# A post-norm transformer layer on one core: maxima rows turned by a transposing DMA, and block 0's output products cut in column halves

## The chip, the cores and the metric

The kernel runs on one core of one Trainium2 chip. The metric is device time in microseconds (us) of one execution; lower is better. Five engines work side by side, each through its own queue in program order: PE (TensorE, matrix products; it reads SBUF and writes the eight banks of PSUM), ACT (ScalarE), DVE (VectorE), POOL (GpSimd) and SP (SyncE), which here only issues DMAs. They wait for each other by semaphores alone.

## The reference

`x` is 2 x 1024 x 512. The layer is attention with residual and layer norm, then a feed-forward stage with residual and layer norm. Only the attention matters here:

```python
qk = (x @ Wqk_w.T + Wqk_b).reshape(b, n, H, E, 2)      # H = 8 heads, E = 8
scores = jnp.einsum('bhqd,bhkd->bhqk', q, k)           # 1024 x 1024 for each head
attn = jax.nn.softmax(scores, axis=-1) / 64 ** 0.5
out = jnp.einsum('bhsl,bhlv->bhsv', attn, v)           # heads joined, then out @ Wo_w.T + Wo_b
x = _layernorm(x + attention(x)); x = _layernorm(x + ffn(x))
```

The feed-forward part has int4 weights with a scale for each group of 128 inputs, and an inner width of 1792. Any true maximum may be taken off a row of scores before the exponential; the kernel takes it off inside the product of the scores, as three more rows of operands.

## The kernel before

The 2048 tokens are four blocks `u` of 512. The eight heads are two groups of four (`NG = 2`), so there are eight groups `f = 2u + g`. A group has eight steps, one for each 128 keys; a step `n` (0 to 63; group `f` starts at step `8f`) has two pairs of heads, `pair` 0 and 1.

**First pass.** `first_pass` (L1040) computes scores of 128 queries by 512 keys into a ring of three PSUM banks (4, 5, 7; `RING`), and DVE reduces each to a maximum (`reduce`, L1356, recorded at L1361). There are 32 such products for each group, 256 in all, and they run ahead of the second pass: 46 come before step 0, then two behind each pair (`firsts_at`), until step 52. When a group's 32 maxima are there, DVE combines them (`combine`, L1364, recorded at L1371) into `mx`.

**Maxima into rows.** POOL splits `mx` into three half-precision parts `mp` (`split_max`, L577). PE turns them at pair 1 of step `8f - 3` (`turn_maxima`, L1057), ACT copies the turned rows out of PSUM to `mrows` (`max_out`, L829), and SP writes them by two DMAs (`max_rows`, L454, recorded at L466) into the operand rows of the group's queries (`qs`). The first scores of group `f`, at step `8f`, wait for that (`s_mld`, L1119).

**Second pass.** For each pair PE computes `scores` (L1112, recorded at L1132) into one of two alternating pairs of banks (0/1 and 2/3), ACT takes the exponential of both banks (`exps`, L814), and PE multiplies by the values one step later, in two halves of the queries (`av`, L1149, recorded at L1161), in bank 6.

**Turns.** Some other uses share the scores' two bank pairs, each in its place in the alternation (`turns_at`, L280): `M` (maxima), `avT` (the sums of group `f`, turned at step `8f + 9`, L1092; ACT copies them, POOL divides them in `normalise`, L660), and for block 0 `attT` (step 20, L1100) and the two output products `wo` (steps 22 and 23, L1108), each copied by ACT into `wob` (L842). In the step behind a turn the first-pass products go ahead of the scores (`firsts_ahead`). From step 53 (`DRAIN`) on the first pass is over and the products of blocks 1 and 2 use banks 4 and 7 instead.

**POOL's order** is written out by hand (L680 on): for each `f` from 2, `normalise(f - 2)`, `split_max(f)`, additions of the bias, loads of the weights (`load_weights`), and behind `f = 3` the four additions of block 0's attention to `x1` (`add_attention`, L646, recorded at L651). **SP's order** too: `max_rows(1)`, twelve DMAs that place rows of the second batch, the load of half of `x` (L483, 2 MB), `max_rows(2)`, the load of the other half (L489), `max_rows(3)`, and so on.

Of the kernel before, what the change touches and what calls it, by code (L numbers as in the profile page):

```python
# [16 lines left out]
F32 = mybir.dt.float32  # L17
# [40 lines left out]
def build(nc, x, xT, wqkT, bqk, wvT, bv, woT, bo, gq, gs, uq, us, dq, ds, ds_next, spread, out):  # L58
    ctx = ExitStack()
    with ctx:  # L60
# [76 lines left out]
        mp = sb("mp", [P, 2, 3 * HG * BT], F16)  # L137
        mrows = sb("mrows", [3 * HG * BT, 2, P], F16)
# [58 lines left out]
        s_m0 = sem("first_max_turn_read")  # L197
        s_of = sem("turn_full")
# [81 lines left out]
        def turns_at(n, pair):  # L280
# [3 lines left out]
            f, r = divmod(n + 3, KT)  # L284
            if r == 0 and f < NB * NG:
                return [("M", f, 0)]
            f, r = divmod(n - 9, KT)
# [3 lines left out]
            if r == 4:  # L291
                return [("attT", 0, 0)]
# [4 lines left out]
        WO_AT = (6, 7)  # L297
# [127 lines left out]
        def _(sp):  # L425
# [110 lines left out]
        def _(pool):  # L536
# [24 lines left out]
            nc.gpsimd.memset(stack[1][:].bitcast(F32), 0.0).then_inc(s_fill, 1)  # L561
            pool.wait_ge(s_fill, 4)
# [14 lines left out]
            def split_max(f):  # L577

                part = [mp[:, f % 2, :].rearrange("p (j i q) -> p i j q", j=2, i=3)[:, i, :, :] for i in range(3)]
                top = mx[:, f % 2, :].rearrange("p (j q) -> p j q", j=2)  # L580
                rest = mres[:].rearrange("p (j q) -> p j q", j=2)
                pool.wait_ge(s_mxc, f + 1)
# [97 lines left out]
            for f in range(2, NB * NG):  # L680
                normalise(f - 2)
                split_max(f)
# [8 lines left out]
                if f == 3:  # L691
                    for t in range(BT):
                        add_attention(0, t)
# [65 lines left out]
        def _(act):  # L759
# [63 lines left out]
            def first_max_out():  # L823

                act.wait_ge(s_rf, ring_count("M", 0))
                nc.scalar.activation(mrows[:, 0, :], ring_bank("M", 0)[0:3 * HG * BT, :].bitcast(F16)[:, 0:P],
                                     ACT.Copy).then_inc(s_m0, 1)

            def max_out(f):  # L829

                act.wait_ge(s_of, turn_count["M", f, 0])
                if f >= 2:
                    act.wait_ge(s_mld[f % NG], 16 * 2 * (f // NG))
                src = bank[shared_banks("M", f, 0)][0:3 * HG * BT, :].bitcast(F16)[:, 0:P]
                nc.scalar.activation(mrows[:, f % 2, :], src, ACT.Copy).then_inc(s_read, 1)
# [20 lines left out]
            def turn_out(kind, u, k):  # L856
# [6 lines left out]
                if kind == "M":  # L863
                    max_out(u)
# [111 lines left out]
        def _(pe):  # L976
# [80 lines left out]
            def turn_maxima(f, dst):  # L1057

                pe.wait_ge(s_mrow, f + 1)
                return nc.tensor.transpose(dst[0:3 * HG * BT, :].bitcast(F16)[:, 0:P], mp[:, f % 2, :], ident16[:])  # L1060
# [580 lines left out]
```

## Time and profile before

| | |
|---|---|
| median of 3 runs | 515.65 us (515.52 to 516.02) |
| the profiled execution | 515.38 us |
| its span, first to last instruction | 513.5 us |
| mean granted TensorE clock | 0.996 of full speed |
| PE busy | 499.5 us |
| DVE busy | 408.8 us |
| ACT busy | 406.8 us |
| POOL busy | 282.9 us |

The attention's second pass runs from about 50 us to about 211 us of the span, the feed-forward stage from there to the end. A row such as "L1161 PE MATMUL ... x832" groups instructions by line; on PE `x8` in a row stands for four fp32 products, which are recorded twice.

### The profile page before, as it was taken

The numbers are of one execution on the slowest core, as the hardware profiler recorded it, in microseconds if no ns is written. First come the engines' busy times: TensorE is split into PE (matmuls) and PEld (weight loads), VectorE is DVE, ScalarE is ACT, GpSimd is POOL, SyncE is SP. The second block draws the span as 40 slices with busy tenths as digits, with TensorE's granted clock in tenths as the row PEclk, the third lists the DMA queues.
The fourth block names the chain that finished last, engine by engine and source line by source line (L and its number), as shares of the span: only waits on it lengthen the run. The fifth ranks groups of instructions, "written<-read, shape, count | busy, mean of one in ns | idle before, by whom it ended". The sixth has DMA issues, their size and how long they took to land.

```text
span 513.5 us, 8164 instructions
## 1 busy us (share of the span) xinstructions
PE 499.5 (97%) x2986; PEld 194.3 (38%) x2986; DVE 408.8 (80%) x688; ACT 406.8 (79%) x569; POOL 282.9 (55%) x330
## 2 busy tenths in 40 slices
PE   8999999999999999999999999999999999999994
PEld 3222233323333322334444444444444444444441
DVE  2799999989999996478778778778668666788676
ACT  1523889988998889868888888888888888888883
POOL 9200094854744444072664686676885874748741
PEclk9999999999999999999999999999999999999998
DMA  6510018953720007500031121130020020000022
GB/s 194 158 48 19 8 54 210 263 106 73 110 43 2 2 5 164 226 1 0 8 56 21 22 41 22 21 63 1 1 82 1 1 84 0 2 0 1 0 82 82
DMA packets 30151, 29.21 MB, mean 57 GB/s; under 512 B 19488, under 2 KB 21920, under 8 KB 29856
## 3 DMA queue, kind: packets, MB, share of 16 engines
q1 hardware_dynamic: 26544, 22.41, 15.2%
q0 software_dynamic: 3424, 6.03, 6.6%
q8 instruction: 23, 0.38, 0.3%
q10 hardware_dynamic: 144, 0.26, 0.1%
q14 instruction: 16, 0.13, 0.1%
HBM read 24.37 MB, written 4.23 MB: 56 GB/s over the span
## 4 chain that ended last, share of the span: by engine, by line
PE 88%; DVE 5%; ACT 3%; issue 1%; DMA 1%; SPq 0%; POOLq 0%; POOL 0%; DVEq 0%
PE ps L1184 19%; PE ps L1172 19%; PE ps L1263 18%; PE ps L1161 10%; PE ps L1054 8%; PE ps L1132 6%; PE ps L984 3%; ACT pbuf L814 3%; DVE mxh L1361 2%; PE ps L1108 1%; PE ps L1144 1%; DMA arena<-xT 1%; PE ps L1036 1%; PE ps L994 1%; PE ps L1092 1%
## 5 line engine op out<-in xcount | busy, mean ns | idle before, releaser
L1361 DVE TENSOR_REDUCE mxh<-ps 128x1 f32<-128x512 f32 x256 | 157.4, 683 | 4.9 <-PE ps L1054 4.0
L814 ACT ACTIVATE pbuf<-ps,gamma 128x1024 f32<-128x1024 f32 x128 | 137.2, 1115 | 15.4 <-PE ps L1132 12.2
L907 ACT ACTIVATE ps<-ps,ratio 128x512 f32<-128x512 f32 x167 | 105.9, 659 | 41.4 <-PE ps L1172 38.6
L1263 PE MATMUL ps<-wd,stack 128*128 128x512 f16 x440 | 129.7, 379 | 0.0
L1184 PE MATMUL ps<-arena,wu 128*128 128x512 f16 x448 | 115.3, 379 | 0.0
L1172 PE MATMUL ps<-arena,wg 128*128 128x512 f16 x448 | 115.3, 379 | 0.1
L1542 DVE TENSOR_TENSOR ps<-ps,stack 128x512 f32<-128x512 f32 x128 | 87.9, 695 | 32.2 <-PE ps L1263 30.3
L913 ACT ACTIVATE ps<-ps,ratio 128x512 f32<-128x512 f32 x156 | 99.0, 659 | 5.4 <-PE ps L1184 1.1
L709 POOL CAST stack<-pbuf 128x512 f16<-128x512 f32 x55 | 33.5, 609 | 74.4 <-DVE pbuf L1517 74.4
L1542 DVE TENSOR_TENSOR ps<-ps,pbuf 128x512 f32<-128x512 f32 x76 | 52.6, 696 | 23.2 <-PE ps L1263 22.4
L1161 PE MATMUL ps<-pbuf,arena 128*32 128x256 f32 x832 | 66.5, 391 | 0.5 <-ACT avt L821 0.2
L711 POOL TENSOR_TENSOR stack<-pbuf,stack 128x512 f16<-128x512 f32 x55 | 63.6, 1156 | 4.5
L1172 PEld LDWEIGHTS ps<-arena,wg 128*128 128x128 f16 x448 | 43.5, 98 | 54.4 <-issue 1.7
L1184 PEld LDWEIGHTS ps<-arena,wu 128*128 128x128 f16 x448 | 43.4, 98 | 54.2 <-DVE pbuf L1517 2.7
L1263 PEld LDWEIGHTS ps<-wd,stack 128*128 128x128 f16 x440 | 43.0, 98 | 52.1 <-DVE ps L1542 0.4
L1054 PE MATMUL ps<-stack 64*128 64x512 f16 x256 | 60.8, 382 | 1.3 <-DVE mxh L1361 0.6
L1132 PE MATMUL ps<-stack 64*128 64x512 f16 x256 | 50.6, 385 | 0.8 <-ACT pbuf L814 0.5
L1517 DVE SCALAR_TENSOR_TENSOR pbuf<-ps,scales,pbuf 128x512 f32<-128x512 f32 x56 | 41.9, 748 | 6.2 <-PE ps L1184 6.1
L921 ACT ACTIVATE pbuf<-ps,scales 128x512 f32<-128x512 f32 x56 | 38.1, 680 | 0.2 <-PE ps L1172 0.2
L1054 PEld LDWEIGHTS ps<-stack 64*128 64x128 f16 x256 | 20.9, 93 | 40.5 <-DVE mxh L1361 34.2
L583 POOL CAST mp<-mx 128x16 f16<-128x16 f32 x8 | 1.6, 196 | 55.0 <-DVE mx L1371 55.0
L1132 PEld LDWEIGHTS ps<-stack 64*128 64x128 f16 x256 | 12.3, 93 | 48.2 <-issue 32.1
(133 smaller groups left out, 412.7 us busy)
## 6 DMA issues: line engine op xcount, KB each, us to landing
arena<-xT SPq DMA_DIRECT2D x16, 256.0 KB, 5.8
x<-x SPq DMA_DIRECT2D x2, 2048.0 KB, 9.8
out<-x SPq DMA_DIRECT2D x3, 1024.0 KB, 4.2
stack<-down_ratios SPq DMA_DIRECT2D x1, 2048.0 KB, 10.3
wg<-gq POOLq DMA_DIRECT2D x4, 448.0 KB, 8.1
wu<-uq POOLq DMA_DIRECT2D x4, 448.0 KB, 7.4
wd<-dq POOLq DMA_DIRECT2D x2, 896.0 KB, 10.8
pbuf<-down_ratios SPq DMA_DIRECT2D x1, 1536.0 KB, 6.3
```

Source lines behind the costliest of these rows:

```text
L711: nc.gpsimd.tensor_tensor(mparts[:, 1, t % NM, :], sg[t % 2], mparts[:, 0, t % NM, :], ALU.subtract)\
L814: nc.scalar.activation(pbuf[:, pi % 4, :].rearrange("p (a n) -> p a n", a=2), ps[:, at:at + 2, :], ACT.Exp, scale=gamma[:, n // (ALL // B) ...
L907: nc.scalar.activation(gbank[t % 2], gbank[t % 2], ACT.Copy, scale=gr[:, t % G, c:c + 1])\
L913: nc.scalar.activation(ubank[t % 2], ubank[t % 2], ACT.Copy, scale=ur[:, t % G, c:c + 1])\
L1054: nc.tensor.matmul(ring_bank("first", n), qs[b][rows, k, t, qt * P:(qt + 1) * P], ks[b][rows, t, half * TB:(half + 1) * TB], start=True, s ...
L1132: mm = nc.tensor.matmul(bank[at + j], ks[b][rows, t, kt * P:(kt + 1) * P], qs[b][rows, k, t, :], start=True, stop=True)
L1161: mm = nc.tensor.matmul(bank[AVB][j * VC:(j + 1) * VC, lo:hi], vst[b][:, kt, g * HG + j, :], pbuf[:, (2 * n + j // 2) % 4, (j % 2) * TB + ...
L1172: mm = nc.tensor.matmul(gbank[t % 2], wg[:, c, i * P:(i + 1) * P], x1v[blk][:, a, c, :, :], start=(c == 0 and a == 0), stop=(a == 1), skip ...
L1184: mm = nc.tensor.matmul(ubank[t % 2], wu[:, c, i * P:(i + 1) * P], x1v[blk][:, a, c, :, :], start=(c == 0 and a == 0), stop=(a == 1), skip ...
L1263: mm = nc.tensor.matmul(bank[k], mparts[:, a, t % NM, k * P:(k + 1) * P], wd[:, i, :], start=(i == 0 and a == 0), stop=(a == 1), skip_grou ...
L1361: nc.vector.tensor_reduce(mxh[:, f % 2, qh, half:half + 1], ring_bank("first", n), AX.X, ALU.max)\
L1542: nc.vector.tensor_tensor(dst, bank[k], by, ALU.mult).then_inc(s_dr[k], 1)
```

## The change

There are four edits.

1. For groups 1 to 7 PE's turn of the maxima and ACT's copy are gone. `mp` and `mrows` are widened to 128 x 128 for each of two slots (POOL zeroes `mp` once at the start), and SP turns them by a transposing DMA ahead of the two writes. It waits for that DMA before it issues the writes.
2. `avT` moves from step `8f + 9` to step `8f + 10`, `attT` of block 0 from step 20 to 22, its `wo` products from steps 22 and 23 to 23 and 27.
3. Each of these two products is computed in halves of 256 columns, with a pair of first-pass products between them, and in the steps around it the order of scores, sums and first-pass products is written out by hand.
4. POOL's last two additions of block 0's attention move from `f = 3` to `f = 4`, between `normalise(2)` and `split_max(4)`.

```diff
@@ turns_at
-            f, r = divmod(n + 3, KT)
-            if r == 0 and f < NB * NG:
-                return [("M", f, 0)]
-            f, r = divmod(n - 9, KT)
+            f, r = divmod(n - 10, KT)
             if r == 0 and 0 <= f < LASTF:
                 return [("avT", f, 0)]
             r = n - STEPS
-            if r == 4:
+            if r == 6:
                 return [("attT", 0, 0)]
...
-        WO_AT = (6, 7)
+        WO_AT = (7, 11)
@@ SP, max_rows(f)
                 if f:
-                    sp.wait_ge(s_read, out_count["M", f, 0])
+                    sp.wait_ge(s_mrow, f + 1)
+                    if f >= 2:
+                        sp.wait_ge(s_mld[g], 16 * 2 * u)
+                    sp.dma_start_transpose(mrows[:, f % 2, :], mp[:, f % 2, :]).then_inc(s_mt, 16)
+                    sp.wait_ge(s_mt, 16 * f)
@@ POOL
+            nc.gpsimd.memset(mp[:].bitcast(F32), 0.0).then_inc(s_pad, 1)
+            pool.wait_ge(s_pad, 1)
...
             for f in range(2, NB * NG):
                 normalise(f - 2)
+                if f == 4:
+                    for t in range(2, BT):
+                        add_attention(0, t)
                 split_max(f)
...
                 if f == 3:
-                    for t in range(BT):
+                    for t in range(2):
                         add_attention(0, t)
@@ PE
+            def half_product(k, part):
+                if part == 0:
+                    i = shared_index["wo", 0, k]
+                    wait_shared_read(pe, *shared[i - 2])
+                    pe.wait_ge(s_wo, 16)
+                    wait_attT(pe, 0)
+                at, cols = shared_banks("wo", 0, k), slice(part * D // 2, (part + 1) * D // 2)
+                for j in range(2):
+                    rows = slice(j * HD, (j + 1) * HD)
+                    mm = nc.tensor.matmul(bank[at + j][:, cols], attT[rows, k * P:(k + 1) * P], wo_s[rows, cols],
+                                          start=True, stop=True)
+                if part:
+                    mm.then_inc(s_of, 1)
...
+            PRODUCT = [STEPS + at for at in WO_AT]
             for n in range(DRAIN):
+                if n in PRODUCT:
+                    k = PRODUCT.index(n)
+                    firsts(n, 0)
+                    scores(n, 0)
+                    av(n - 1, 0)
+                    scores(n, 1)
+                    firsts(n, 1)
+                    half_product(k, 0)
+                    firsts(n + 1, 0)
+                    half_product(k, 1)
+                    continue
+                if n - 1 in PRODUCT:
+                    scores(n, 0)
+                    av(n - 2, 1)
+                    firsts(n, 1)
+                    av(n - 1, 0)
+                    scores(n, 1)
+                    firsts(n + 1, 0)
+                    av(n - 1, 1)
+                    continue
+                if n - 2 in PRODUCT:
+                    scores(n, 0)
+                    if n % KT != 1:
+                        av(n - 1, 0)
+                    firsts(n, 1)
+                    scores(n, 1)
+                    if n % KT == 1:
+                        av(n - 1, 0)
+                    av(n - 1, 1)
+                    continue
@@ DVE, combine(f)
-                if f == 2:
-                    dve.wait_ge(s_rf, ring_count("M", 0))
-                elif f > 2:
-                    dve.wait_ge(s_of, turn_count["M", f - 2, 0])
+                if f >= 2:
+                    dve.wait_ge(s_mrow, f - 1)
```

In what follows rows of the changed kernel carry its own line numbers: L1058 is a first-pass product, L1149 scores, L1178 sums, L1124 a half product, L460 the transposing DMA, L469 the writes.

**PE, steps 22 to 25 of block 0's products.** `stack1` marks the first pass (second batch), `stack0` the scores. Before, from the sums in step 22:

```order
L1161 MATMUL ps<-pbuf,arena 32x256 x4
L1132 MATMUL ps<-stack0 128x512 x2
L1054 MATMUL ps<-stack1 128x512 x2
L1108 MATMUL ps<-wo_s,attT 128x512 x2
L1161 MATMUL ps<-pbuf,arena 32x256 x4
L1054 MATMUL ps<-stack1 128x512 x2
L1132 MATMUL ps<-stack0 128x512 x2
```

Of the change, from the second pair of step 23:

```order
L1149 MATMUL ps<-stack0 128x512 x2
L1058 MATMUL ps<-stack1 128x512 x2
L1124 MATMUL ps<-wo_s,attT 128x256 x2
L1058 MATMUL ps<-stack1 128x512 x2
L1124 MATMUL ps<-wo_s,attT 128x256 x2
L1149 MATMUL ps<-stack0 128x512 x2
L1178 MATMUL ps<-pbuf,arena 32x256 x4
L1058 MATMUL ps<-stack1 128x512 x2
L1178 MATMUL ps<-pbuf,arena 32x256 x4
```

The whole product with sums behind it between two first-pass pairs has become two halves on either side of a pair, and the sums stand behind the next step's scores. In step 25, the second step of a group, both halves of the sums come together:

```order
L1149 MATMUL ps<-stack0 128x512 x2
L1058 MATMUL ps<-stack1 128x512 x2
L1149 MATMUL ps<-stack0 128x512 x2
L1178 MATMUL ps<-pbuf,arena 32x256 x8
L1149 MATMUL ps<-stack0 128x512 x2
L1058 MATMUL ps<-stack1 128x512 x2
```

Eight sum products and two scores now stand between two first-pass pairs there.

**SP, groups 1 to 3.** The `8x4x...` rows place the second batch, `x1<-x` are the two loads of 2 MB. Before:

```order
L466 DMA stack0<-mrows 3x8x128 x2
L376 DMA stack1<-x1 8x4x512 x8
L373 DMA stack1<-x1 8x4x1024 x4
L483 DMA x1<-x 128x8x512
L466 DMA stack0<-mrows 3x8x128 x2
L489 DMA x1<-x 128x8x512
```

Of the change:

```order
L460 DMA_TRANSPOSE mrows<-mp 128x128
L469 DMA stack0<-mrows 3x8x128 x2
L375 DMA stack1<-x1 8x4x512 x8
L372 DMA stack1<-x1 8x4x1024 x4
L486 DMA x1<-x 128x8x512
L460 DMA_TRANSPOSE mrows<-mp 128x128
L469 DMA stack0<-mrows 3x8x128 x2
L492 DMA x1<-x 128x8x512
```

Each pair of writes has a transposing DMA ahead of it; group 2's is issued behind the first 2 MB load, on the same queue, and the second load behind its writes.

**POOL, groups 3 and 4.** `inv`, `left` and `att` are `normalise(2)`, `mp` and `mres` are `split_max`. Before:

```order
L617 DMA wu<-uq 128x1792 x4
L651 TENSOR_TENSOR x1<-wob,x1 128x512 x4
L667 TENSOR_TENSOR inv<-av_s,minus 128x16
L670 TENSOR_TENSOR left<-av_s,inv 128x16
L672 TENSOR_SCALAR left<-left 128x16
L674 TENSOR_TENSOR inv<-inv,left 128x16
L677 TENSOR_TENSOR att<-av_s,inv 128x4x32
L583 CAST mp<-mx 128x2x8
```

Of the change:

```order
L628 DMA wu<-uq 128x1792 x4
L662 TENSOR_TENSOR x1<-wob,x1 128x512 x2
L678 TENSOR_TENSOR inv<-av_s,minus 128x16
L681 TENSOR_TENSOR left<-av_s,inv 128x16
L683 TENSOR_SCALAR left<-left 128x16
L685 TENSOR_TENSOR inv<-inv,left 128x16
L688 TENSOR_TENSOR att<-av_s,inv 128x4x32
L662 TENSOR_TENSOR x1<-wob,x1 128x512 x2
L594 CAST mp<-mx 128x2x8
```

Two of the four additions now stand directly ahead of the split of group 4's maxima.

## Rows read from the trace of the kernel before

**Rows 1.** The page: busy time of each engine.

```profile
PE 499.5 (97%) x2986; PEld 194.3 (38%) x2986; DVE 408.8 (80%) x688; ACT 406.8 (79%) x569; POOL 282.9 (55%) x330
```

**Rows 2.** Timeline of DVE, 40 to 190 us: start, length, instruction, [idle before, releaser].

```profile
62.67 13.36 DVE L1361 TENSOR_REDUCE mxh<-ps 128x1 f32<-128x512 f32 x22
76.25 6.20 DVE L1361 TENSOR_REDUCE mxh<-ps 128x1 f32<-128x512 f32 x10 [0.21 <-PE ps L1054]
82.48 0.18 DVE L1371 TENSOR_TENSOR mx<-mxh 128x16 f32<-128x16 f32 x1
...
102.39 0.18 DVE L1371 TENSOR_TENSOR mx<-mxh 128x16 f32<-128x16 f32 x1
...
109.69 2.61 DVE L1361 TENSOR_REDUCE mxh<-ps 128x1 f32<-128x512 f32 x4 [0.83 <-PE ps L1054]
113.14 3.81 DVE L1361 TENSOR_REDUCE mxh<-ps 128x1 f32<-128x512 f32 x6 [0.83 <-PE ps L1054]
...
124.84 0.18 DVE L1371 TENSOR_TENSOR mx<-mxh 128x16 f32<-128x16 f32 x1
...
184.56 0.18 DVE L1371 TENSOR_TENSOR mx<-mxh 128x16 f32<-128x16 f32 x1
```

**Rows 3.** Timeline of PE, steps 22 and 23.

```profile
105.77 0.39 PE L1054 MATMUL ps<-stack 64*128 64x512 f16 x2
...
106.36 0.64 PE L1161 MATMUL ps<-pbuf,arena 128*32 128x256 f32 x8
106.93 0.39 PE L1132 MATMUL ps<-stack 64*128 64x512 f16 x2
107.16 0.38 PE L1054 MATMUL ps<-stack 64*128 64x512 f16 x2
107.64 1.13 PE L1108 MATMUL ps<-wo_s,attT 64*128 64x512 f32 x4
108.70 0.64 PE L1161 MATMUL ps<-pbuf,arena 128*32 128x256 f32 x8
109.27 0.39 PE L1054 MATMUL ps<-stack 64*128 64x512 f16 x2
```

**Rows 4.** The chain of waits in order of time, 58 to 120 us: start, length, what.

```profile
74.71 0.61 PE ps L1092 x4
...
90.35 0.32 PE ps L1132 x2
```

**Rows 5.** The chain of waits from 184 us on.

```profile
184.73 2.39 DVE st L1391 x4
...
187.98 1.13 PE ps L1108 x4
```

**Rows 6.** Timelines of POOL and ACT: additions of block 0, and behind group 4's maxima.

```profile
111.39 4.99 POOL L651 TENSOR_TENSOR x<-wob,x 128x512 f32<-128x512 f32 x4
125.92 0.22 POOL L589 TENSOR_TENSOR mp<-mres,mp 128x16 f16<-128x16 f32 x1
128.01 0.26 ACT L835 ACTIVATE mrows<-ps 48x128 f16<-48x128 f16 x1
131.25 2.00 POOL L620 DMA_DIRECT2D wd<-dq  x2 [5.12 <-DMA stack<-mrows]
```

**Rows 7.** DMA: transposes of 128 x 1024 (L498, landing), and packets from 195.5 to 196.5 us.

```profile
DMA to landing us min/median/max: 3.0/3.1/3.6
DMA packets 734, 0.18 MB, mean 180 GB/s; under 512 B 734, under 2 KB 734, under 8 KB 734
```

**Rows 8.** DMA: the first load of `x` (issue, landing), group 2's writes, packets 87 to 88 us.

```profile
78.73 0.45 SPq L483 DMA_DIRECT2D x<-x  x1
DMA to landing us min/median/max: 10.6/10.6/10.6
85.93 1.51 SPq L466 DMA_DIRECT2D stack<-mrows  x2
DMA packets 140, 0.22 MB, mean 216 GB/s; under 512 B 37, under 2 KB 37, under 8 KB 140
```

More of the change, by code:

```diff
@@ L136, in build @@
         mres = sb("mres", [P, HG * BT], F32)
-        mp = sb("mp", [P, 2, 3 * HG * BT], F16)
-        mrows = sb("mrows", [3 * HG * BT, 2, P], F16)
+        mp = sb("mp", [P, 2, P], F16)
+        mrows = sb("mrows", [P, 2, P], F16)
         ident16 = sb("ident16", [P, P], F16)
@@ L197, in build @@
         s_m0 = sem("first_max_turn_read")
+        s_pad = sem("max_parts_padded")
+        s_mt = sem("max_parts_turned_by_dma")
         s_of = sem("turn_full")
@@ L577, in split_max @@
             def split_max(f):
-                part = [mp[:, f % 2, :].rearrange("p (j i q) -> p i j q", j=2, i=3)[:, i, :, :] for i in range(3)]
+                part = [mp[:, f % 2, 0:3 * HG * BT].rearrange("p (j i q) -> p i j q", j=2, i=3)[:, i, :, :] for i in range(3)]
                 top = mx[:, f % 2, :].rearrange("p (j q) -> p j q", j=2)
                 rest = mres[:].rearrange("p (j q) -> p j q", j=2)
+                if f < 2:
+                    pool.wait_ge(s_pad, 1)
+                elif f == 2:
+                    pool.wait_ge(s_m0, 1)
+                else:
+                    pool.wait_ge(s_mt, 16 * (f - 2))
                 pool.wait_ge(s_mxc, f + 1)
@@ L825, in first_max_out @@
                 act.wait_ge(s_rf, ring_count("M", 0))
-                nc.scalar.activation(mrows[:, 0, :], ring_bank("M", 0)[0:3 * HG * BT, :].bitcast(F16)[:, 0:P],
+                nc.scalar.activation(mrows[0:3 * HG * BT, 0, :], ring_bank("M", 0)[0:3 * HG * BT, :].bitcast(F16)[:, 0:P],
                                      ACT.Copy).then_inc(s_m0, 1)
[L829 to L835, printed above, removed]
             def wo_out(u, k):
@@ L862, in turn_out @@
                     wo_out(u, k)
-                if kind == "M":
-                    max_out(u)
             act.wait_ge(s_const, 1)
@@ L1055, in first_pass, with turn_first_maxima @@
                                  ks[b][rows, t, half * TB:(half + 1) * TB], start=True, stop=True).then_inc(s_rf, 1)
-            def turn_maxima(f, dst):
-                pe.wait_ge(s_mrow, f + 1)
-                return nc.tensor.transpose(dst[0:3 * HG * BT, :].bitcast(F16)[:, 0:P], mp[:, f % 2, :], ident16[:])
+            def turn_first_maxima(dst):
+                pe.wait_ge(s_mrow, 1)
+                return nc.tensor.transpose(dst[0:3 * HG * BT, :].bitcast(F16)[:, 0:P], mp[:, 0, 0:3 * HG * BT], ident16[:])
             def ring_use(kind, n):
@@ L1071, in ring_use @@
                 else:
-                    turn_maxima(0, ring_bank("M", 0)).then_inc(s_rf, 1)
+                    turn_first_maxima(ring_bank("M", 0)).then_inc(s_rf, 1)
             def turn(kind, u, k):
@@ L1085, in turn @@
                 dst = bank[at]
-                if kind == "M":
-                    mm = turn_maxima(u, dst)
-                elif kind == "avT":
+                if kind == "avT":
                     pe.wait_ge(s_ave, u + 1)
@@ L1212, in _, with firsts @@
                     piece(p)
+            def firsts(n, pair):
+                for use in ring_uses_at(n, pair):
+                    ring_use(*use)
+            PRODUCT = [STEPS + at for at in WO_AT]
             for n in range(DRAIN):
+                if n in PRODUCT:
[28 more added lines that the diff above has]
+                    continue
                 after_group_start = n % KT == 1
```

## The prediction

> **What bounds the kernel now.** The page comes first. PE is busy for nearly the whole span [rows 1], which invites the thought that everything taken off PE is gained. The timeline of DVE contradicts that from 62 to 184 us, the stretch that the change touches. DVE makes 22 reductions in 13.36 us [rows 2]; the last alone takes 0.68, so they start 0.604 us apart, back to back, and a pair needs 1.21. A group without block 0's turns takes 82.48 to 102.39, 19.91 us, with a single idle time of 0.21 in it [rows 2]. The group with them takes 102.39 to 124.84, 22.45 us, with 0.83 twice, each time for a first-pass product [rows 2]. So in this stretch DVE sets the pace, and PE's work counts only where it brings a pair of first-pass products so late that DVE runs dry. Over the six groups from 62.6 to 184.56 us at most 6 x 0.21 + 2.54 = 3.8 us can be won.
>
> How late may PE be? The pair at 105.77 was followed by one at 107.16, 0.18 later than DVE's 1.21, and that one by the pair at 109.27, 0.90 later [rows 3]; of the 1.08 DVE idled 0.83 [rows 2]. The ring thus covers 0.25 us. Lateness below that costs nothing, and is paid back by pairs that come sooner than 1.21.
>
> **Edit 1, PE and ACT.** It takes off seven turns of 0.24 and seven copies of 0.26 [rows 6]. In groups 1 to 6 DVE does not idle at these turns [rows 2], so I take nothing. The last, at step 53, lies behind the first pass. There PE and ACT would be 0.7 us sooner at the scores of step 54, but the chain shows who waits: DVE's statistics, 184.73 to 187.12, then the copy of block 1's turned attention, then the product at 187.98 [rows 5]. It starts no sooner, so again nothing.
>
> **Edit 1, the way of the maxima.** Before, group 4's went from the combination at 124.84 over POOL (done 126.14) to ACT (done 128.27), and the writes had landed by 131.25 [rows 6]: 2.98 us for the writes. Now a transposing DMA of time T stands in place of PE and ACT. The known transposes carry 128 x 1024 halves, 256 KB in 256-byte packets, and land in 3.1 us [rows 7]; 734 packets pass in a microsecond [rows 7], so 1024 take 1.4. Ours has 128 packets, 1.2 us fewer: T = 1.9, with 3.1 as its upper end if the time lies elsewhere. The sum is 1.30 + 1.9 + 2.98 = 6.2 us from the combination. The group's first scores come 90.35 - 82.48 = 7.87 us behind it [rows 2, 4]. For most groups the change is hidden, with 1.7 us to spare; at T = 3.1, with 0.5.
>
> Group 2 is another matter. Its parts are ready at 83.8 us, while the 2 MB load of `x` issued at 78.73 is under way; that lands 10.6 us later, at 89.3 [rows 8]. The transpose stands behind it on SP's queue. If each DMA engine takes them in order, and 128 rows spread over all engines, it lands at 89.3 at the earliest; the writes then land at 92.3, and the scores of step 16, due at 90.35 [rows 4], wait 1.97 us. PE stands, the first-pass products behind the scores too, and after 0.25 DVE: **+1.7 us**. At least nothing, if the transpose is not held up; at most 1.2 more (T = 3.1 with none of it hidden behind the load).
>
> **Edit 2.** `avT` (0.61) [rows 4] leaves the second step of a group, where PE's order is already late by 0.1, for the third. The 0.21 of idle time it makes [rows 2] should shrink to about 0.13, counted in the manner of edit 3. Five groups outside block 0's products: **-0.5 us**, between 0 and the full -1.05.
>
> **Edit 3.** The time between the starts of two first-pass pairs is a sum of pieces: a first-pass pair or scores 0.22 (107.16 less 106.93), or 0.31 if a single-precision product follows (0.32 for the scores of [rows 4]), half of the sums 0.57, a whole product 1.06 (107.64 to 108.70) [rows 3], so a half 0.53, `avT` 0.61. In the new order the distances from the second pair of step 22 on are: 1.24, 1.32, 0.84, 1.72, 1.10, 1.10, 1.99, 1.11, 1.48, 1.32, 0.84, 1.72, 1.10, 1.76, 1.32. The 1.72 is half a product, scores and half the sums between two pairs. The 1.99 is step 25, with both halves of the sums and two scores; I add 0.2 there, since ACT has copied a product just before and is late with the old sums. Counted against 1.21, with lateness up to 0.25 free and never below zero, DVE idles 0.26, 0.56, 0.17, 0.11, 0.26, 0.44 and 0.11: 1.9 us. Before it was 22.45 - 19.91 + 0.21 = 2.75. **-0.85 us**; it can be nothing if ACT's copies (1.02 each) get in the way, and -1.3 if the 0.56 goes.
>
> **Edit 4.** Two additions of 1.25 [rows 6] now delay the split of group 4's maxima by 2.5 us, so they reach the rows 8.7 us behind the combination. The scores of step 32 are due after 7.87, plus the idle times of edit 3 that now lie behind that combination (0.26 + 0.44 + 0.11): 8.7. Even, so nothing; at T = 3.1 PE is 1.2 late and DVE idles about 0.8 us with the pair's cover partly used. POOL's one more memset at the start is covered by its wait for DVE there.
>
> **The sum.** +1.7 - 0.5 - 0.85 = +0.35, rounded to **+0.4 us**. The profiled execution took 515.38 us (span 513.5), so its like would take 515.8. That execution lay 0.27 below the median; against the median of 515.65 I predict **516.0 us**. A measurement of this kernel can tell a difference of 0.2%, 1.03 us, so the forecast is no change.
>
> **Rivals.**
> - *The transpose does not queue behind the load.* Group 2's writes, issued at 85.93, had 37 small packets moving between 87 and 88 us, with large ones still beside them [rows 8]. That speaks for a free way. But these writes have 24 rows each and may lie on few engines, and the load's landing at 89.3 needs the slowest of them. Then the stall is gone: -1.35 us, **514.3 us**. The Trainium skill, "DMA: Bandwidth & Descriptors", section on queues, rings and completion order, has one ring for each issuing queue on each DMA engine, consumed in order; by that rule this rival is out and the stall stands. The trace doesn't settle it.
> - *The small transpose is as slow as the large (slower than before).* The place is SP's wait between transpose and writes. With T = 3.1, group 2 loses 1.2 us more and group 4 0.8: +2.4 us, **518.0 us**. It turns the sign to slower from T = 2.5 on, where group 2 alone adds 0.6. Against it speak the packets of rows 7. The Trainium skill, "VectorE: DVE Perf Modes", rules for kernel authors, speaks against the change itself: a 128 x 128 transpose belongs on TensorE where PSUM will do, and on the DMA crossbar otherwise. By that rule the new way is the longer one, as it is in this rival.
> - *The halves win nothing.* ACT's copy and the doubled sums of step 25 take back the 0.85: +1.2 us, **516.9 us**. For it speaks that PE's work from step 20 to 28, 8 x 2.22 us of pairs and 3.1 of turns, exceeds DVE's 19.7 whatever its order.
>
> **How the numbers follow.** The forecast gets a chance of 0.42, the free way 0.28, the slow transpose 0.18, the useless halves 0.12. The forecast's own spread is about 0.8 us either side: 0.28 within 0.2%, 0.04 faster, 0.10 slower. The free way lies just past the limit: 0.20 faster, 0.08 the same. The slow transpose gives 0.16 slower and 0.02 the same, the useless halves 0.09 slower and 0.03 the same. Together: faster 0.24, same 0.41, slower 0.35. The range holds 514.2 (the free way with its spread) to 518.2 (the slow transpose).
>
> **What the changed profile would show.** DVE's timeline should have one idle time of about 1.7 us near 90 us, at the first-pass product of step 16, with PE waiting for SP's writes; no such wait at steps 8, 24, 40, 48 and 56; group 3, from its combination to the next, near 20.8 us, and its neighbour 20.5; idle times of 0.1 to 0.6 there instead of 0.83 twice; other groups 0.1 us shorter. The transposing DMA should land in 1.9 us, that of group 2 at 89.3. The prediction is wrong if step 16 doesn't wait, if other groups' scores do, if block 0's turns leave more than 2.5 us of idle time, or if the end no longer moves with the combination of the last group (184.56 us).

## The result, and the profile after

| | before | after |
|---|---|---|
| median | 515.75 us, 7 runs (515.52 to 516.02) | 518.22 us, 7 runs (516.67 to 519.89) |
| ratio after/before | | 1.0051, 95% interval 1.0038 to 1.0065 |
| profiled execution | 515.38 us, span 513.5 | 519.43 us, span 517.4 |

The change makes the kernel 0.5% slower. The forecast was no change, 516.0 us; 518.22 lies 0.02 above the top of the range. The spread matters too: the kernel before stays within 0.5 us in these seven runs (1.3 to 2.5 us in the larger sets measured with the experiments), the changed one within 3.2, and its time goes with the mean granted clock of the run: 0.997 in the runs of 516.67 and 516.83 us, 0.991 to 0.994 in the five of 517.97 to 519.89. The profiled execution is one of the long ones, so it shows 4.05 us of difference where the medians show 2.5.

The page after: PE's clock in 40 slices, and DVE's reductions, whose idle time was 4.9 us before.

```profile
PEclk9999999799999999999999999999999999999999
L1416 DVE TENSOR_REDUCE mxh<-ps 128x1 f32<-128x512 f32 x256 | 157.3, 683 | 8.9 <-PE ps L1058 8.1
```

The timeline of DVE, which answers to [rows 2]:

```profile
62.42 0.18 DVE L1424 TENSOR_TENSOR mx<-mxh 128x16 f32<-128x16 f32 x1
...
82.17 0.18 DVE L1424 TENSOR_TENSOR mx<-mxh 128x16 f32<-128x16 f32 x1
93.65 1.29 DVE L1416 TENSOR_REDUCE mxh<-ps 128x1 f32<-128x512 f32 x2 [2.93 <-PE ps L1058]
95.62 1.29 DVE L1416 TENSOR_REDUCE mxh<-ps 128x1 f32<-128x512 f32 x2 [0.68 <-PE ps L1058]
97.60 1.29 DVE L1416 TENSOR_REDUCE mxh<-ps 128x1 f32<-128x512 f32 x2 [0.69 <-PE ps L1058]
99.23 3.68 DVE L1416 TENSOR_REDUCE mxh<-ps 128x1 f32<-128x512 f32 x6 [0.34 <-PE ps L1058]
...
106.92 0.18 DVE L1424 TENSOR_TENSOR mx<-mxh 128x16 f32<-128x16 f32 x1
117.05 3.68 DVE L1416 TENSOR_REDUCE mxh<-ps 128x1 f32<-128x512 f32 x6 [0.22 <-PE ps L1058]
121.34 1.29 DVE L1416 TENSOR_REDUCE mxh<-ps 128x1 f32<-128x512 f32 x2 [0.61 <-PE ps L1058]
122.82 1.29 DVE L1416 TENSOR_REDUCE mxh<-ps 128x1 f32<-128x512 f32 x2 [0.20 <-PE ps L1058]
124.30 3.81 DVE L1416 TENSOR_REDUCE mxh<-ps 128x1 f32<-128x512 f32 x6 [0.19 <-PE ps L1058]
128.14 0.20 DVE L1424 TENSOR_TENSOR mx<-mxh 128x16 f32<-128x16 f32 x1
131.39 13.52 DVE L1416 TENSOR_REDUCE mxh<-ps 128x1 f32<-128x512 f32 x22 [0.58 <-PE ps L1058]
...
148.91 0.18 DVE L1424 TENSOR_TENSOR mx<-mxh 128x16 f32<-128x16 f32 x1
...
188.42 0.18 DVE L1424 TENSOR_TENSOR mx<-mxh 128x16 f32<-128x16 f32 x1
```

From one combination to the next: the group behind 82.17 takes 24.75 us where it took 19.91, the two with block 0's turns 21.22 and 20.77 where they took 22.45 and 19.91 [rows 2], the others 19.75 or 19.76. So the whole loss, 4.84, lies between 82 and 107 us; the rest gives back 0.37 in block 0's two groups and about 0.15 in each other.

Why DVE ran dry there stands in SP's timeline (the load, the transposing DMA, the writes of group 2) and in PE's around step 16:

```profile
78.63 0.45 SPq L486 DMA_DIRECT2D x<-x  x1
83.56 1.14 SPq L460 DMA_TRANSPOSE mrows<-mp  x1
89.79 1.54 SPq L469 DMA_DIRECT2D stack<-mrows  x2
```

```profile
89.30 0.64 PE L1178 MATMUL ps<-pbuf,arena 128*32 128x256 f32 x8
92.58 0.61 PE L1149 MATMUL ps<-stack 64*128 64x512 f16 x2 [2.64 <-DMA stack<-mrows]
...
93.54 1.08 PE L1178 MATMUL ps<-pbuf,arena 128*32 128x256 f32 x8
```

The transposing DMA, issued at 83.56, lands just before 89.79, 6.2 us later; five of the other six land in 2.3 to 2.4, group 5's in 3.25. The writes go out then, and PE stands 2.64 us for them. What follows was not in the prediction: the same instructions are slower when PE starts again (sums 1.08 instead of 0.64, scores 0.61 instead of 0.39). The stretches of the trace show why (busy time of each engine, then the granted clock, DMA share, GB/s):

```profile
90.00:91.00 1.00, 0.00 (x0) 0.00 (x0) 0.72 (x2) 0.22 (x1) 1.00 (x1) 1.00 0.00 0
91.00:92.00 1.00, 0.00 (x0) 0.00 (x0) 0.00 (x0) 0.00 (x0) 1.00 (x1) 0.89 0.03 7
92.00:94.00 2.00, 1.42 (x12) 0.33 (x12) 0.35 (x1) 0.77 (x1) 2.00 (x1) 0.50 0.45 137
94.00:96.00 2.00, 2.00 (x20) 0.33 (x12) 1.32 (x3) 1.14 (x2) 2.00 (x5) 0.50 0.87 298
96.00:98.00 2.00, 2.00 (x18) 0.36 (x14) 1.31 (x3) 1.65 (x3) 0.33 (x1) 0.50 1.06 401
98.00:99.00 1.00, 1.00 (x10) 0.22 (x10) 0.89 (x2) 1.00 (x2) 0.00 (x0) 0.70 1.06 283
```

PE stood from 90 us on, the clock fell in the stretch from 91 to 92, and it was at 0.50, the 1.2 GHz level, until past 98. But the DMA engines were also nearly or quite full from 94 us on (the second load of `x`, and from 97.9 us the weights' load too), so the slow rows had two possible causes.

**Theories.** Q: the transposing DMA waits for the load of `x`, which costs one stall at step 16. C: the stall makes the clock fall, which costs again. Rival D: the slowness behind the stall is contention with the DMAs. Rival T: the way by DMA is too long in every group. Open besides: what the other parts are worth, and whether it is the queue or the DMA engines that hold the transposing DMA.

### The profile page after: what moved, and what is told of

The parts are those of the page before. It is cut to its first block, busy times and chain, and to the rows that moved or that the text cites. A ratio compares the mean times of both kernels' runs of the same rounds, so it can differ in the third digit from the quotient of the medians.

```text
span 517.4 us, 8170 instructions
## 1 busy us (share of the span) xinstructions
PE 501.2 (97%) x2987; PEld 194.5 (38%) x2987; DVE 408.9 (79%) x688; ACT 406.6 (79%) x562; POOL 283.5 (55%) x331
## 4 chain that ended last, share of the span: by engine, by line
PE 85%; DVE 5%; ACT 3%; DMA 2%; issue 2%; POOL 1%; SPq 0%; POOLq 0%; DVEq 0%; ACTq 0%
PE ps L1201 19%; PE ps L1189 19%; PE ps L1318 18%; PE ps L1178 9%; PE ps L1058 7%; PE ps L1149 5%; PE ps L988 3%; DVE mxh L1416 2%; ACT pbuf L828 2%; DMA mrows<-mp 2%; PE ps L1161 1%; PE ps L1040 1%; PE ps L998 1%; PE ps L1210 1%; PE ps L1110 1%
## 5 line engine op out<-in xcount | busy, mean ns | idle before, releaser
L911 ACT ACTIVATE ps<-ps,ratio 128x512 f32<-128x512 f32 x167 | 105.9, 659 | 41.4 <-PE ps L1189 38.6
L1178 PE MATMUL ps<-pbuf,arena 128*32 128x256 f32 x832 | 67.4, 397 | 0.9 <-ACT pbuf L828 0.3
L1058 PE MATMUL ps<-stack 64*128 64x512 f16 x256 | 61.3, 388 | 1.3 <-DVE mxh L1416 0.6
L1149 PE MATMUL ps<-stack 64*128 64x512 f16 x256 | 51.0, 392 | 3.5 <-DMA stack<-mrows 2.6
L1058 PEld LDWEIGHTS ps<-stack 64*128 64x128 f16 x256 | 20.7, 94 | 39.4 <-DVE mxh L1416 35.7
L678 POOL TENSOR_TENSOR inv<-av_s,minus 128x16 f32<-128x16 f32 x6 | 17.6, 2930 | 31.8 <-ACT av_s L860 31.8
L1149 PEld LDWEIGHTS ps<-stack 64*128 64x128 f16 x256 | 12.5, 93 | 53.8 <-issue 34.3
```

The costliest lines, as they stand in the source:

```text
L911: nc.scalar.activation(gbank[t % 2], gbank[t % 2], ACT.Copy, scale=gr[:, t % G, c:c + 1])\
L1058: nc.tensor.matmul(ring_bank("first", n), qs[b][rows, k, t, qt * P:(qt + 1) * P], ks[b][rows, t, half * TB:(half + 1) * TB], start=True, s ...
L1149: mm = nc.tensor.matmul(bank[at + j], ks[b][rows, t, kt * P:(kt + 1) * P], qs[b][rows, k, t, :], start=True, stop=True)
L1178: mm = nc.tensor.matmul(bank[AVB][j * VC:(j + 1) * VC, lo:hi], vst[b][:, kt, g * HG + j, :], pbuf[:, (2 * n + j // 2) % 4, (j % 2) * TB + ...
```

## The experiments

"Before" is always the kernel before, measured together with the version.

**1. The load early.** The changed kernel with one line moved.

```diff
             sp.dma_start(bo_s, bo).then_inc(s_bo, 16)
+            sp.dma_start(x1[:, 0:8, :], x[0:8].rearrange("t p n -> p t n")).then_inc(s_x[0], 16)
             max_rows(1)
...
             place_rows(sp, 1)
-            sp.dma_start(x1[:, 0:8, :], x[0:8].rearrange("t p n -> p t n")).then_inc(s_x[0], 16)
             max_rows(2)
```

> The changed kernel, with one DMA moved: the first 2 MB load of x goes out ahead of group 1's maxima (at about 50 us, where DMA is idle) instead of at 78.6 us. Theory Q (group 2's transposing DMA stands behind that load on SP's queue, and its stall at step 16 is the loss): the transpose of group 2 lands 2.3 us after its issue like the others, no wait at step 16, group 2 takes 19.75 us from combination to combination instead of 24.75, and the time is 519.4 - 5.0 = 514.4 to 514.8 us, faster than before by 0.2%. Rival T (the transposing way is too long by itself, load or no load): DVE still idles over 1 us at step 16 and the time stays above 516.

Measured: 514.87 us, ratio 0.9987 (0.9978 to 0.9995). SP's timeline now, with the same issue time of the transposing DMA:

```profile
83.56 1.12 SPq L460 DMA_TRANSPOSE mrows<-mp  x1
85.87 1.54 SPq L469 DMA_DIRECT2D stack<-mrows  x2
```

It lands in 2.3 us, step 16 doesn't wait, the group takes 19.74 us and the clock stays at 1.0. Against the kernel before of the same call the median goes from +2.47 (518.22 less 515.75) to -0.48 (514.87 less 515.35), so the load's place alone was 2.95 us. Theory Q stands, and T falls: every group outside block 0's takes 19.74 or 19.75.

**2 and 3. Edit 1 alone, and edit 1 with the early load.** The kernel before with edit 1 (transposing DMA, no turns of the maxima), PE's order otherwise as before; the second has the moved line of experiment 1 as well.

```diff
@@ turns_at, from the kernel before
-            f, r = divmod(n + 3, KT)
-            if r == 0 and f < NB * NG:
-                return [("M", f, 0)]
@@ max_rows, POOL, combine
+  as in the change
```

> The kernel before with edit 1 alone (transposing DMA for groups 1 to 7; PE's order of turns, products and POOL's additions as before). Theory Q: the whole loss is in edit 1, through group 2: group 2 takes about 24.9 us instead of 19.91, all other groups as before, time 518 to 520 us, that is above the changed kernel by the 0.8 us that edits 2 to 4 gave. Rival E (the new order of PE's work costs time): this kernel is faster than the changed one, 516 to 517.5.

> The kernel before with edit 1 alone, and with the first 2 MB load of x ahead of group 1's maxima. Theory Q: without the stall edit 1 is worth nothing, because PE's turn of the maxima lay under DVE's reductions: 515.7 us, within 0.2 us of before, every group as before. Rival P (PE's and ACT's 0.24 and 0.26 us count): 1 us or more below before.

Measured: 518.46 us, ratio 1.0057 (1.0041 to 1.0074), and 514.58 us, ratio 0.9988 (0.9979 to 0.9996). Edit 1 alone has the whole loss. Its part in the gain shows in the timeline of DVE of the version with the early load, block 0's groups:

```profile
102.03 0.17 DVE L1368 TENSOR_TENSOR mx<-mxh 128x16 f32<-128x16 f32 x1
108.73 2.61 DVE L1360 TENSOR_REDUCE mxh<-ps 128x1 f32<-128x512 f32 x4 [0.45 <-PE ps L1055]
112.18 3.81 DVE L1360 TENSOR_REDUCE mxh<-ps 128x1 f32<-128x512 f32 x6 [0.84 <-PE ps L1055]
...
123.87 0.17 DVE L1368 TENSOR_TENSOR mx<-mxh 128x16 f32<-128x16 f32 x1
...
143.66 0.18 DVE L1368 TENSOR_TENSOR mx<-mxh 128x16 f32<-128x16 f32 x1
```

Two groups in 41.63 us against 42.36 before [rows 2]: the first of the two idle times of 0.83 has shrunk to 0.45, since PE, without the turn at step 21, is less late. Three of the other four groups take 19.78 to 19.80, 0.12 less than before. So the turns that I costed at nothing were worth about 1.2 us over the stretch (41.63 holds 0.73 less, of which 0.12 is the second group's; four more groups give 0.12 each), and edits 2 to 4, added in experiment 1, bring nothing on top: block 0's two groups take 42.02 there, 0.39 more, and the others 19.74, 0.05 less. One group of this version took 20.41, with its transposing DMA landing 4.3 us after its issue; that belongs to the last section.

**4. PE kept busy.** The changed kernel, with twelve products of no use before step 16's wait; they write a bank that the scores overwrite.

```diff
+FILL = 12
...
+                at = shared_banks("scores", n, pair)
+                if n == 16 and pair == 0:
+                    wait_shared_read(pe, *shared[shared_index["scores", n, pair] - 2])
+                    for _ in range(FILL):
+                        nc.tensor.matmul(bank[at], still[:, 0:P], still[:], start=True, stop=True)
                 if kt == 0 and pair == 0:
                     pe.wait_ge(s_mld[g], 16 * 2 * (u + 1))
-                at = shared_banks("scores", n, pair)
```

> The changed kernel, with twelve products of 128 x 512 halves (0.22 us each at full clock, 2.6 us together) on PE ahead of the scores of step 16, while it would wait for the maxima; they go into the bank that the scores then overwrite. Theory C (PE stands still for 2.6 us, the granted clock falls to 0.50 from 92 to 98.5 us, and that adds idle times of 0.68, 0.69 and 0.34 us on DVE behind the stall): the stall of DVE at step 16 stays, at 2.3 to 2.9 us, the clock stays at 1.00, the three idle times go, and the time is 516.7 us, with a spread under 0.5 us where the changed kernel spread from 516.7 to 519.9. Rival D (the products behind the stall are slow because the second load fills the DMA engines then): products of 0.6 us and the three idle times stay, with a clock row of 1.00 or not, and the time stays near 518.

Measured: 516.89 us (516.75 to 517.32), ratio 1.0031 (1.002 to 1.0042). PE's timeline, then one of the stretches:

```profile
89.83 2.76 PE L1140 MATMUL ps<-still 128*128 128x512 f16 x12
92.77 0.39 PE L1154 MATMUL ps<-stack 64*128 64x512 f16 x2 [0.18 <-DMA stack<-mrows]
```

```profile
96.00:98.00 2.00, 1.95 (x22) 0.64 (x22) 2.00 (x4) 1.97 (x3) 0.53 (x2) 1.00 1.02 391
```

The scores start as late as before, the DMA share is as high, and yet they take 0.39 and the clock stays at 1.00; DVE idles 2.74 once and the group takes 22.59 us. So C, not D: the stall costs 22.59 - 19.74 = 2.85 us, the clock 24.75 - 22.59 = 2.16 in the profiled execution. Between medians, each against the kernel before of its call, it is 2.02 (from -0.48 to +1.54) and 0.93 (to +2.47). Part of the gap between the two prices of the stall is the choice of execution: the one profiled in experiment 1 is the fastest of its eleven, 0.73 below their median. The spread shrinks from 3.2 us in seven runs to 0.57 in six, all with mean clocks from 0.996 to 0.998, so most of it came from the clock.

**5 and 6. The load on ACT's queue**, in the changed kernel and in the kernel before.

```diff
@@ ACT
                     exps(n, pair)
+                    if (n, pair) == (11, 1):
+                        act.dma_start(x1[:, 0:8, :], x[0:8].rearrange("t p n -> p t n")).then_inc(s_x[0], 16)
@@ SP
-            sp.dma_start(x1[:, 0:8, :], x[0:8].rearrange("t p n -> p t n")).then_inc(s_x[0], 16)
```

> The changed kernel with one edit: the first 2 MB load of x is issued by ACT, behind its exponentials of step 11 (about 79 us), instead of by SP. The load's bytes and its time stay, only the queue it stands on is another. If the small transposing DMA of group 2 was held up because it stood behind the load on SP's own queue, it now lands about 2.3 us after its issue at 83.56, the scores of step 16 do not wait, and the time is that of the kernel with the early load: 0.4 to 0.8 us below the kernel before, 3.3 below the changed one. If what held it up is the load's hold on the DMA engines themselves, whatever the queue, it lands near 89.5 again, step 16 waits some 2.6 us, PE's granted clock drops to a half for 6 us, and the time stays 2.5 us above the kernel before. In between (landing at 86.5 to 88) the writes would land by 91 at the latest and cost at most 0.6 us.

> The kernel before with the first load of x issued by ACT at about 79.7 us instead of by SP. Its writes of group 2's maxima (ordinary DMAs, no transpose) are issued at 85.93, alone on SP's queue. If a DMA engine serves the other queue only once its work for the first is through, whatever the kind of DMA, none of their small packets moves before 87, as with the transposing DMA. If only a transposing DMA waits for the others, their small packets move between 86 and 87 us beside the load's large ones. The time is that of the kernel before either way, within 0.5 us.

Measured: 518.34 us, ratio 1.0057 (1.0044 to 1.0069), and 515.31 in one run. The queue makes no difference to the changed kernel. The transposing DMA is issued at 83.76, alone on SP's queue, and lands as late as before, 6.2 us after; PE stands 2.59 us at step 16:

```profile
83.76 1.13 SPq L460 DMA_TRANSPOSE mrows<-mp  x1
89.94 1.54 SPq L469 DMA_DIRECT2D stack<-mrows  x2
```

Packets by queue (count, MB, share of 16 engines), from 86 to 87 us and from 87 to 88; q1 is SP's, q10 the load on ACT's:

```profile
q10 hardware_dynamic: 186, 0.38, 103.4%
...
q10 hardware_dynamic: 128, 0.24, 63.0%
q1 hardware_dynamic: 126, 0.03, 12.8%
```

No packet of q1 moves before 87.3 us, 3.5 us after the issue; in experiment 1, with the engines idle, the first moves after 1.1 (the issue is at 83.56, one packet moves before 84.7 and 121 from there to 84.9). So the load holds the DMA back by 2.4 us at its start, and it begins as the load's own packets get fewer, although its queue is free. What holds it up is the work that the engines already have, not the order on SP's queue.

Experiment 6 can't tell whether ordinary writes are held up too. They are issued at 85.78 and their first packets move at 87.1, 1.3 us later; but in experiment 9, where the load is long over, the same writes are issued at 85.98 and their first packets move at 87.3, also 1.3 us later. They came too late in the load to be delayed by it. The changed kernel's own trace does have ordinary DMAs behind a load on another queue: POOL's loads of weights (q0), issued from 94.04 us on beside the second load of `x` (q1). The packets are those from 97 to 98 us:

```profile
94.04 2.29 POOL L625 DMA_DIRECT2D wg<-gq  x4
...
q1 hardware_dynamic: 183, 0.37, 99.5%
q0 software_dynamic: 4, 0.01, 7.1%
```

The first packet of q0 moves after 97.9, 3.9 us behind the issue; where the engines are idle (the kernel before, issued at 109.16) it moves after 1.3. So the wait is not peculiar to the transposing DMA.

The Trainium skill, "DMA: Bandwidth & Descriptors", section on queues, rings and completion order, lets each engine alternate between the queues packet by packet, with 9 to 17 descriptors in a typical packet and 64 at most. With turns of the typical length the trace does not agree: in the 2.4 us that the transposing DMA was held back, the load moved 186 of the profile's 2 KB packets a microsecond, some 28 on each engine. A turn near the maximum would agree, since 2 MB in 2 KB packets is 64 for each of 16 engines (both are estimates, and they take one such packet for one descriptor). No run here tells how long a turn is.

**7. Whole products.** The kernel of experiment 1 with the branches for `PRODUCT` and its two next steps removed, and `turn("wo", 0, k)` at steps 23 and 27 in the general loop.

> The changed kernel with the early load of x, and with block 0's two output products whole again, each at its step (23 and 27) as one piece in the order of all other turns; the sums' late places around them go too. Two groups (3 and 4) contain them; they took 42.02 us together with halves and the early load. If the halves are worth what the prediction took for them, 0.85 us, the two groups take 42.9 and the kernel 515.7, with idle times of DVE of about 0.8 twice. If the halves win nothing (the prediction's rival), the two groups take 42.0 within 0.2 and the time is that of the kernel with the early load, 514.9. If they even cost (the version with the turn by DMA alone had 41.63), the two groups take 41.6 and the time is 514.5.

Measured: 514.93 us, ratio 0.9986 (0.9977 to 0.9995). DVE's combinations around the two groups:

```profile
101.66 0.18 DVE L1386 TENSOR_TENSOR mx<-mxh 128x16 f32<-128x16 f32 x1
...
111.21 3.81 DVE L1378 TENSOR_REDUCE mxh<-ps 128x1 f32<-128x512 f32 x6 [0.84 <-PE ps L1058]
...
143.76 0.18 DVE L1386 TENSOR_TENSOR mx<-mxh 128x16 f32<-128x16 f32 x1
```

42.10 us against 42.02 with halves: the halves of edit 3 win 0.08. Two idle times of 0.84 stand against five of 0.22, 0.61, 0.20, 0.19 and 0.58. Whole products at steps 22 and 23 took 41.63 (experiment 3), so moving them to steps 23 and 27 did not help: with the rest of edits 2 and 4 it cost 0.47.

**8. A recombination that failed.** Edit 1, the early load, `avT` a step later, attention turned at step 22, whole products at steps 23 and 24.

> A kernel put together from the parts: the maxima's way by DMA and the early load of x, avT a step later as in the change, block 0's attention turned at step 22, its two products whole at steps 23 and 24, and none of the rest (no halves, no late additions on POOL). If avT a step later is worth 0.1 us in each group, as the prediction took, it is 0.5 us below the version without it, 514.1. If with the turn of the maxima gone the slot is free anyway, the groups without block 0's turns stay at 19.75 to 19.8 us and the time is 514.6 within 0.2.

Measured: 515.91 us, ratio 1.0009 (1.0000 to 1.0018). Missed: `avT` a step later gains next to nothing (19.74 to 19.82 a group against 19.79), and behind two products in a row PE waits for ACT's copy of the second, whose banks it needs, before the second scores of step 25:

```profile
116.73 0.39 PE L1131 MATMUL ps<-stack 64*128 64x512 f16 x2 [1.09 <-ACT wob L845]
```

DVE then idles 1.31, and block 0's two groups take 43.02.

**9. Control: the kernel before with the early load.**

> The kernel before with nothing but the early load of x (issued at about 50 us instead of 78.7), a control. If the 0.6 to 0.8 us that the versions with the early load gained on the kernel before come from the maxima's way, this one is the same as the kernel before within 0.2 us. If they come from the load's new place (less traffic beside group 2), this one gains them too: 514.7.

Measured: 515.47 us against 515.4, ratio 0.9999 (0.9990 to 1.0008). The load's place is worth nothing by itself in the kernel before; the gains with it are the change's, and by experiment 3 those of edit 1.

**10. Part of the filling.** Experiment 4 with 4 products instead of 12.

> The changed kernel with 4 products without use on PE before the scores of step 16, where an earlier run had 12: they cover some 0.9 of the 2.6 us that PE stands there, and 1.7 us of standing is left. DVE's idle time at step 16 stays near 2.8. If the clock falls whatever PE still stands, the granted clock is a half from 92 to 98 again and the time is that of the changed kernel, 2.5 to 3 us above the kernel before. If 1.7 us of standing is short enough, the clock stays at 1.0 and the time is that with 12 products, 1.5 above. In between, a shorter stretch at the half clock than the changed kernel's 6.5 us, and idle times of DVE of 0.7 once instead of twice.

Measured: 517.03 us (516.14 to 517.77), ratio 1.0025 (1.0016 to 1.0033): the time of the twelve. The twelve runs have mean clocks from 0.996 to 0.999, so their spread of 1.6 us is not the clock's. In the profiled one PE stood 1.88 us and the clock stayed at 1.00:

```profile
93.15 0.39 PE L1154 MATMUL ps<-stack 64*128 64x512 f16 x2 [1.88 <-DMA stack<-mrows]
```

**11 and 12. Halves far apart.** Edit 1 and the early load, in the kernel before's order; each half product is a turn of its own.

```diff
-            if r == 4:
+            if r == 5:
                 return [("attT", 0, 0)]
-        WO_AT = (6, 7)
+        WO_AT = (7, 11, 13, 15)
@@ ACT, wo_out for block 0; PE's product likewise
+                    cols, k = slice(k % 2 * D // 2, (k % 2 + 1) * D // 2), k // 2
+                    nc.scalar.activation(wob[:, 2 * k:2 * k + 2, cols], ps[:, at:at + 2, cols], ACT.Copy)
@@ POOL, experiment 11: two additions at f = 3, two at f = 4; experiment 12:
+                if f == 5:
+                    for t in range(BT):
+                        add_attention(0, t)
```

> A version meant to beat both kernels: the maxima's way by DMA and the early load of x, the order of the kernel before on PE, but block 0's two products split into four turns of one column half each, at steps 23, 27, 29 and 31, each with its own copy by ACT (attention turned at step 21; the later rows' additions behind the split of group 4). A half adds 0.53 us to PE's order; two steps give back 0.4 (PE needs 2.22 a step, DVE 2.42) and 0.25 is covered. If PE's order alone decides, DVE idles 0.3 at each half at the most, and the two or three groups with them take 0.5 to 1.0 us less than the 41.63 of the whole products at steps 22 and 23: 513.8 to 514.1. If ACT's two shorter copies or the sums behind them set the time, it is 514.6 as before, or more.

> The run before last with one thing mended: POOL's four additions of block 0's attention stand behind the split of group 5's maxima and the bias of block 2, so that POOL is free at 113 to 118 us for the normalising of the third group's sums, and splits group 4's maxima as soon as they are combined (122.6). In that run POOL had waited for the product at step 27 first, the split came 5.5 us late, PE waited 2.9 us at step 32 and DVE idled 3.09. If that was all, the idle time of 3.09 goes to under 0.3, groups 3 and 4 take 40.6 to 41.1 us together, and the time is 0.7 to 1.3 us below the kernel before of the same call, some 0.6 below the version with whole products. If POOL is late at group 5 or 6 now (additions of 2.5 and 5 us ahead of a normalising), a wait of PE turns up at step 40 or 48 instead and the gain is gone. If the shorter copies of ACT cost, there are idle times of 0.3 or more behind steps 27 to 31.

(The text on record for experiment 12 speaks of experiment 11 as the run before last.) Experiment 11: 517.9 us, ratio 1.0042 (1.0027 to 1.0057). The products did what they should (the first group 20.56 us), but POOL stood in its order at an addition that needs the product of step 27, with the normalising and the split of group 4 behind it. POOL's addition, and then PE's scores of step 32:

```profile
121.40 2.52 POOL L662 TENSOR_TENSOR x<-wob,x 128x512 f32<-128x512 f32 x2 [10.09 <-ACT wob L850]
```

```profile
134.25 0.39 PE L1141 MATMUL ps<-stack 64*128 64x512 f16 x2 [2.88 <-DMA stack<-mrows]
```

Experiment 12: **514.06 us (513.46 to 514.41) against 515.58, ratio 0.9965 (0.9952 to 0.9978)**, faster than both kernels. DVE's timeline has nothing left but small idle times:

```profile
101.93 0.18 DVE L1375 TENSOR_TENSOR mx<-mxh 128x16 f32<-128x16 f32 x1
114.64 1.29 DVE L1367 TENSOR_REDUCE mxh<-ps 128x1 f32<-128x512 f32 x2 [0.16 <-PE ps L1059]
116.13 6.32 DVE L1367 TENSOR_REDUCE mxh<-ps 128x1 f32<-128x512 f32 x10 [0.21 <-PE ps L1059]
122.48 0.17 DVE L1375 TENSOR_TENSOR mx<-mxh 128x16 f32<-128x16 f32 x1
...
142.99 0.18 DVE L1375 TENSOR_TENSOR mx<-mxh 128x16 f32<-128x16 f32 x1
...
182.60 0.17 DVE L1375 TENSOR_TENSOR mx<-mxh 128x16 f32<-128x16 f32 x1
```

Two groups in 41.06, 0.57 less than with whole products at steps 22 and 23. The last combination comes 1.96 us sooner than in the kernel before [rows 2], and the profiled span is 511.6, 1.9 shorter.

## Why the prediction was wrong

- **What bounds the kernel: right.** The last combination came 3.86 us later than before (188.42 against 184.56 [rows 2]) and the profiled execution was 4.05 longer.
- **The failed step: "PE stands, the first-pass products behind the scores too, and after 0.25 DVE: +1.7 us".** Place, order and cause were right, the size was not. PE's wait was 2.64, not 1.97: the transposing DMA landed near 89.8, not 89.3, and the writes at 92.5. DVE idled 2.93, with no 0.25 taken off. And the term ended there. The fallen clock held DVE up three more times, by 0.68, 0.69 and 0.34. The group lost 4.84 in the profiled execution; experiments 1 and 4 put 2.85 on the stall and 2.16 on the clock, less 0.17 for the turns that are gone, where I had 1.7 and nothing.
- **Why the load held it: half right.** I put it down to order on SP's queue, and the rival of a free way to the absence of such an order. Experiment 5 has no shared queue and the same wait. The 37 small packets between 87 and 88 us [rows 8], which I read as speaking for a free way, say nothing either way: on idle engines the same writes start no sooner, 1.3 us after their issue (experiment 9).
- **T = 1.9 us, upper end 3.1:** 2.3 in five groups, 3.25 in group 5, above my upper end, and hidden in all of them, as predicted. The rival of a slow transpose named 518.0 us, near the measured time, but that is luck: T is 2.3 without a load in its way, and step 32 is 0.13 us late, not 1.2.
- **Edit 1 on PE and ACT, "nothing": wrong by about 1.2 us** over the stretch (experiment 3). I looked only at whether DVE idles at a turn. A turn makes PE late for the next one too. At the end it gave nothing, as predicted: PE waited 0.99 for DVE's copy at 191.85.
- **Edit 2, -0.5:** the groups did become 0.15 to 0.16 shorter each, but edit 1 had 0.12 of that; 0.04 is left for the later `avT`, 0.2 in all.
- **Edit 3, -0.85: wrong.** The halves by themselves are worth 0.08 (experiment 7). Against the old order with edit 1 in place, the new order costs 0.39 in these two groups (42.02 against 41.63). They took 21.22 and 20.77 us, where I had named 20.8 and 20.5. The idle times I listed for the new order add up to 1.9, and those found (0.22, 0.61, 0.20, 0.19, 0.58) to 1.8. But the two groups take 42.02 in experiment 1, which is 2.54 more than twice 19.74: some 0.7 lies in idle times that the list leaves out, most of them too short for a row of their own. For the order before I had taken the whole measured excess (22.45 - 19.91 = 2.54), for the new one a list of idle times without those gaps. Like against like, both are 2.54. The rival of the useless halves had 0.12 of the chance, and it held; that ACT's copies were the reason, as it says, no run shows.
- **Edit 4, even: right.** PE's scores of step 32 start at 136.95, 0.70 behind the start of the sums ahead of them (136.25), where 0.57 is usual: 0.13 late.
- **Sum.** The parts outside group 2 were forecast at -1.35 and gave -0.48 (experiment 1); group 2 was forecast at +1.7 and cost 2.95 between medians. Both errors go the same way: +0.35 became +2.47.

## What to carry to other kernels

Before a small DMA goes onto a path with a deadline, list the large transfers under way at its issue, on every queue: here a 2 MB load held up a small transposing DMA until it was nearly through, whichever engine had issued it, and moving that load 29 us earlier cost nothing. Price a stall of PE with what it does to the clock: 2.6 us of standing cost 2.9 in the profiled execution, and the slower clock behind it 2.2 more (2.0 and 0.9 between medians). When work is spread over time to hide it, move its consumers on in-order engines behind what has a deadline as well; that, not the halves themselves, decided between 517.9 and 514.06 us.

## What the runs showed that I had not expected

- **The clock does not fall every time.** It fell to 0.50 after PE stood 2.64 us in the changed kernel's profile, and not at all after 2.88 us in experiment 11's (granted clock 1.00 in all of its stretches from 130 to 140 us). That kernel's other runs had mean clocks from 0.994 to 0.997 and took 517.37 to 518.41 us, against 516.82 with 0.997 in the profiled one. The Trainium skill, "TensorE: Matmul & The Clock Gate", Part 1, says of the warm-up at a kernel's start that its length varies from run to run of the same kernel; that a fall in mid-kernel also comes in some runs and not in others agrees with it.
- **A half-way fall.** In experiment 2 PE stood 2.42 us, the first scores behind it still took 0.39, and only the next 0.61; the granted clock of its stretches was 0.81 from 92 to 94 us, 0.50 from 94 to 96, 0.83 from 96 to 98.
- **Late packets.** The transposing DMA usually lands 2.3 us after its issue, in which SP's issue takes 1.13. Group 5's took 3.1 to 4.3 us in nine of the eleven versions, and 2.3 in the other two (experiments 4 and 11). In experiment 3, 158 of its packets moved in the microsecond from 146 us, beside an instruction fetch, and two came after 148; that made step 40 wait 0.6 us. That the fetch delayed one engine is only argued: no run took it away. Group 3's took from 2.3 us (the changed kernel) to 4.2 (experiment 4, where POOL's loads of weights, 448 KB each, filled the engines at its issue: 105.9% from 106 to 107 us). So other loads than those of `x` may hold it up; no run moved them.
- **What stays open:** how an engine shares its time between queues. Behind the second load of `x` POOL's packets waited until 97.9 us, but from then on both queues moved packets, 36 and 75 from 98 to 99 us, and the rest of the load took until past 105. Whether they took turns on the same engines the trace's views don't tell.
